# A mixture-of-experts loop on one core: W1 as the stationary operand, loaded per tile; free tags; one jump over skipped rounds; final statistics shared between two engines

## The reference

```python
x = x + attn(layernorm(x))            # 16 heads, bias table added after the softmax, then a layernorm
x = x + cross_attn(layernorm(x), ctx) # 77 context rows, 16 heads, masked
x = x + ffn(layernorm(x))
# ffn: 8 experts, top 2 of softmax(flat @ gate_W), weights normalised to sum 1
out = 0.5 * gelu(flat @ shared_W + shared_b)
for e in range(8):
    h = gelu(flat @ W1[e] + b1[e])                        # (2048,256) @ (256,1024)
    out = out + combine[:, e:e+1] * (h @ W2[e] + b2[e])   # (2048,1024) @ (1024,256)
out = layernorm(out) * gamma + beta
```

## Time and profile before

| | |
|---|---|
| median of 3 runs | 824.73 us (821.93 to 825.29) |
| profiled execution, its own time | 817.05 us |
| its span | 815.2 us |
| PE busy | 741.1 us, 91% |
| DVE, ACT, POOL busy | 363.7, 408.1, 147.5 us |
| mean granted TensorE clock | 0.97 |
| moved to and from HBM | 72.86 MB read, 42.33 MB written |

### The profile page before, as it was taken

One profiled execution on the slowest core, in us unless ns is written; L12 is line 12 of the kernel. 1 busy time (PEld: TensorE's weight loads), 2 busy tenths in 40 slices (PEclk: granted clock), 3 DMA queues, 4 the chain that ended last, 5 costly groups with the idle time before them and its releaser, 6 DMA issues.

```text
span 815.2 us, 17861 instructions
## 1 busy us (share of the span) xinstructions
PE 741.1 (91%) x6677; PEld 431.6 (53%) x6678; DVE 363.7 (45%) x1012; ACT 408.1 (50%) x514; POOL 147.5 (18%) x140
## 2 busy tenths in 40 slices
PE   4978999999999999988998899999999999999820
PEld 2444445454544444434555675767676766767520
DVE  5771220210154452588466543444444444444336
ACT  2746889887898898945564332212111121212104
POOL 2020050010000000200043340333212112121414
PEclk9997999999999999999999989999999999999975
DMA  9577939860203123036339955454444544454444
GB/s 210 148 233 192 318 89 318 277 205 23 81 2 101 39 63 99 3 113 257 117 112 317 331 213 174 102 126 111 120 120 106 123 102 126 99 130 110 73 116 103
DMA packets 81471, 116.21 MB, mean 143 GB/s; under 512 B 11202, under 2 KB 69788, under 8 KB 79066
## 3 DMA queue, kind: packets, MB, share of 16 engines
q1 hardware_dynamic: 73864, 104.27, 41.9%
q0 software_dynamic: 7536, 10.95, 7.6%
HBM read 72.86 MB, written 42.33 MB: 141 GB/s over the span
## 4 chain that ended last, share of the span: by engine, by line
PE 77%; DVE 9%; DMA 6%; ACT 4%; issue 2%; SPq 1%; POOL 1%; ACTq 0%; DVEq 0%; POOLq 0%
PE ps L1853 15%; PE ps L2195 14%; PE ps L2178 14%; PE ps L1830 14%; PE ps L2186 4%; DMA q_parts<-arena 2%; PE ps L2034 2%; DMA x_sb<-in_x 1%; PE ps L1868 1%; PE ps L1990 1%; PE ps L1812 1%; PE ps L1906 1%; DMA sums_by_row<-arena 1%; PE ps L2168 1%; PE ps L2031 1%
## 5 line engine op out<-in xcount | busy, mean ns | idle before, releaser
L847 ACT ACTIVATE arena<-ps 128x1024 f32<-128x1024 f32 x256 | 241.2, 1034 | 35.5 <-PE ps L1853 35.3
L1853 PE MATMUL ps<-arena 99*32 99x512 bf16 x2048 | 162.9, 390 | 3.2 <-issue 2.7
L1830 PE MATMUL ps<-arena 128*32 128x256 f32 x2048 | 159.6, 382 | 0.6 <-issue 0.6
L2195 PE MATMUL ps<-arena,xh_tag 128*128 x560 | 128.4, 383 | 3.0 <-DVE xh_tag L1557 3.0
L2178 PE MATMUL ps<-arena 128*128 x280 | 126.2, 593 | 0.8 <-ACT arena L958 0.5
L2195 PEld LDWEIGHTS ps<-arena,xh_tag 128*128 128x128 f32 x560 | 104.9, 192 | 16.9 <-issue 3.7
L958 ACT COPY arena<-ps 128x256 f32<-128x256 f32 x35 | 13.0, 372 | 195.9 <-PE ps L2168 195.9
L751 POOL DMA_INDIRECT sums_by_row<-arena x39 | 60.2, 1544 | 228.2 <-DVE arena L1579 226.9
L1830 PEld LDWEIGHTS ps<-arena 128*32 128x32 f32 x2048 | 65.3, 111 | 53.1 <-issue 3.3
L1552 DVE TENSOR_TENSOR xh_tag<-ps,xh_tag 128x1024 f32<-128x1024 f32 x35 | 42.9, 1225 | 88.3 <-PE ps L2178 88.3
L2178 PEld LDWEIGHTS ps<-arena 128*128 128x128 f32 x280 | 50.5, 190 | 51.5 <-issue 51.4
(11 more groups left out here) (247 smaller groups left out, 792.2 us busy)
## 6 DMA issues: line engine op xcount, KB each, us to landing
xh_tag<-in_L_ffn_b SPq DMA_DIRECT2D x35, 512.0 KB, 3.7
rows_by_expert<-arena SPq DMA_DIRECT2D x9, 1950.0 KB, 14.8
arena<-in_L_ffn_W SPq DMA_DIRECT2D x16, 1024.0 KB, 10.9
arena<-q_parts SPq DMA_DIRECT2D x90, 128.0 KB, 2.7
arena<-k_parts SPq DMA_DIRECT2D x42, 128.0 KB
q_parts<-arena SPq DMA_DIRECT2D x12, 384.0 KB, 2.5
arena<-rows_by_expert SPq DMA_DIRECT2D x35, 130.0 KB, 2.1
arena<-in_L_ffn_b SPq DMA_DIRECT2D x35, 128.0 KB, 3.0
```

The lines of the kernel that those rows point to most:

```text
L847: nc.scalar.activation(probs_of(stage, h), ps[:, 2 * (u % 2):2 * (u % 2) + 2, :].rearrange("p a n -> p (a n)"), ACT.Exp, scale=float(D) ** ...
L1830: last = nc.tensor.matmul(ps[32 * h:32 * h + 32, 4 + half, at:at + 256], v_grp[n % 2][:, kt, h, :], probs_of(stage, h)[:, 256 * part:256 * ...
L1853: last = nc.tensor.matmul(ps[c:c + 32, 2 * (u % 2) + half, :], k_stk[buf][:, h, P * st + c:P * st + c + 32], q_stk[buf][:, h, 512 * half:5 ...
L2195: last = nc.tensor.matmul(ps[:, 6, 0:D], hid_t[:, k, :], w2_sb[:, bass.ds(e, 1), k, :].squeeze(1), start=(k == 0), stop=(k == HID // P - 1))
```

## The change

W1 is no longer resident. SP loads the W1 of each tile's expert, 1 MB, into one of two buffers (`w1_buf`), as soon as `layer1` two tiles back has ended. `layer1` now takes pieces of W1 as the stationary operand and the tile's turned rows as the moving one, so that the hidden values come out already turned. `turn_hidden`, `sum_hidden` and `turned_hidden` go; b1 becomes a column per 128 hidden values, added within the gelu, which ACT does in eight pieces straight from PSUM, into two alternating `hid_t`. The per-tile broadcast of b1 goes too: all b1 are turned once (`b1_all`) and DVE copies eight columns per tile (`bias1`). `tags` no longer waits for a scatter, since the row numbers that POOL reads are copied to `row_used` in `result`. A conditional round that is not run jumps over all later ones. In front of the loop `keep_busy(1)` becomes `keep_busy(4)`, the later `keep_busy(2)` goes, and the third base store comes after the first two W1 loads. In the last stage three of the six pieces get their sums and squares from ACT's accumulating activations; DVE does the rest with two fused operations for each row tile; POOL has no part.

```diff
-        w1_sb = Region(0).take([P, EXPERTS, KC, HID])
+        r = Region(0)
+        w1_buf = r.take([P, 2, KC, HID])
+        b1_all = r.take([P, EXPERTS, HID // P])
...
             with eng.If_ne(flag, 0):
                 body(i)
+                may_run(on, eng, i + 1, body, counts)
             with eng.If_eq(flag, 0):
-                for s, before_round, step in counts(i):
-                    eng.wait_ge(s, before_round)
-                    eng.sem_inc(s, step)
+                for skipped in range(i, PAIRS):
+                    for s, before_round, step in counts(skipped):
+                        eng.wait_ge(s, before_round)
+                        eng.sem_inc(s, step)
...
-            for e in range(2, EXPERTS - 1):
-                load_w1(e)
+            sp.dma_start(b1_rows, b1.rearrange("e (k p) -> (e k) p", p=P)).then_inc(b1_in, 16)
...
-            for ch in range(3):
+            for ch in range(2):
                 store_base(ch)
...
-                sp.wait_ge(h_sum, j + 1)
-                load_b1(e, buf)
+                sp.wait_ge(h_ps, 2 * j + 2)
+                load_w1(e, buf)
...
-            sp.wait_ge(scattered, 16 * 2 * NT)
             sp.wait_ge(slot_ready, NT // CHUNK + 1)
             for j in range(2):
+                load_w1(expert(j), j)
+            store_base(2)
+            sp.wait_ge(scattered, 16 * 2 * NT)
+            for j in range(2):
                 load_rows(slots_of(j), j)
-                load_b1(expert(j), j)
...
+                add_result((n - 1) % 2, n, row_used[:, (n - 1) % 2:(n - 1) % 2 + 1], sums_set)
...
-            pool.wait_ge(x_shifted, 2 + B)
-            for n in range(LAST):
-                rows = slice(*ROUNDS[n])
-                pool.wait_ge(out_scaled, n + 1)
-                nc.gpsimd.tensor_tensor(x_sb[:, rows, :], x_sb[:, rows, :], y_in[:, rows, :], ALU.add).then_inc(out_ready, 1)
...
-            def activate(n):
-                act.wait_ge(h_sum, n)
-                nc.scalar.activation(hid, hid, ACT.Gelu).then_inc(h_act, 1)
+            def activate(buf, n, free=None):
+                act.wait_ge(b1_ready, n)
+                if free is not None:
+                    act.wait_ge(y_ps, free)
+                for half in range(2):
+                    act.wait_ge(h_ps, 2 * n - 1 + half)
+                    for c in range(4):
+                        k = 4 * half + c
+                        last = nc.scalar.activation(hid_t[:, buf, k, :], ps[:, 4 * buf + half, P * c:P * (c + 1)], ACT.Gelu,
+                                                    bias=b1_col[:, buf, k:k + 1])
+                last.then_inc(h_act, 1)
...
+            def sums(n):
+                act.wait_ge(y_landed[n], 16)
+                first, end = ROUNDS[n]
                 for t in range(first, end):
-                    last = nc.scalar.activation(y_in[:, t, :], y_in[:, t, :], ACT.Identity, scale=rstd[:, t:t + 1], bias=shift[:, t:t + 1])
-                last.then_inc(out_normed, 1)
+                    last = nc.scalar.activation(unread[:, t - first, :], y_in[:, t, :], ACT.Identity, scale=-1.0 / D, accum_out=shift[:, t:t + 1])
+                last.then_inc(out_sums, 1)
+                n_sums[0] += 1
+            def squares(n):
+                act.wait_ge(out_sums, n_sums[0])
+                first, end = ROUNDS[n]
+                for t in range(first, end):
+                    last = nc.scalar.activation(unread[:, t - first, :], y_in[:, t, :], ACT.Square, bias=shift[:, t:t + 1], accum_out=mv[:, t, 1:2])
...
+            act.wait_ge(y_ps, SLOT_TILES)
+            root_of_vector(1, 0)
+            sums(1)
+            root_of_vector(2, 2)
+            squares(1)
+            sums(3)
+            squares(3)
+            root_of_vector(3, 5)
+            sums(4)
+            squares(4)
...
+            def bias1(buf, tile, read=None):
+                e = nc.vector.value_load(tile_expert[0:1, tile], min_val=0, max_val=EXPERTS - 1)
+                if read is not None:
+                    dve.wait_ge(h_act, read)
+                nc.vector.tensor_copy(b1_col[:, buf, :], b1_all[:, bass.ds(e, 1), :].squeeze(1)).then_inc(b1_ready, 1)
...
-                    dve.wait_ge(sums_set, 16 * taken)
...
+                if keep_rows:
+                    nc.vector.tensor_copy(row_used[:, buf:buf + 1], row_at[:, buf:buf + 1])
...
-                    turned_hidden(2 * i + (o + 2))
-                    sum_hidden(o, 2 * i + (o + 3), 16 * i + 32)
-                    tags(o, 2 * i + (o + 3), bass.ds(2 * i + (o + 2), 1), 2 * i + (o + 1),
-                         min(2 * i + (o + 1), 2 * SURE + 1) if may_be_skipped else 2 * i + (o + 1))
+                    bias1(o, bass.ds(2 * i + (o + 2), 1), 2 * i + (o + 1))
+                    dve.wait_ge(xs_ps, 2 * i + (o + 3))
+                    tags(o, 2 * i + (o + 3), bass.ds(2 * i + (o + 2), 1), 2 * i + (o + 1))
...
+            def centred(n, roots=None):
+                if roots is not None:
+                    dve.wait_ge(ln_std, len(LN_TILES) + roots + 1)
+                else:
+                    dve.wait_ge(ln_var, len(LN_TILES) + 1 + D_ROUNDS.index(n) + 1)
+                for t in range(*ROUNDS[n]):
+                    middle, op = (shift[:, t:t + 1], ALU.add) if n in BY_SCALAR else (mv[:, t, 0:1], ALU.subtract)
+                    last = nc.vector.scalar_tensor_tensor(out=y_in[:, t, :], in0=y_in[:, t, :], scalar=middle, in1=ffn_g_sb, op0=op, op1=ALU.mult)
+                link(last)
...
+            def added(n, roots):
...
+                dve.wait_ge(ln_std, len(LN_TILES) + roots + 1)
+                link(nc.vector.reciprocal(rstd[:, rows], rstd[:, rows]))
+                for t in range(*ROUNDS[n]):
+                    last = nc.vector.scalar_tensor_tensor(out=x_sb[:, t, :], in0=y_in[:, t, :], scalar=rstd[:, t:t + 1], in1=x_sb[:, t, :],
+                                                          op0=ALU.mult, op1=ALU.add)
+                last.then_inc(out_scaled, 1)
...
+            dve.wait_ge(x_shifted, 2 + B)
             variances(0)
-            for n in range(LAST):
-                variances(n + 1)
-                scales(n)
-                if n >= 1:
-                    gains(n - 1).then_inc(out_scaled, 1)
-            scales(LAST)
-            gains(LAST - 1).then_inc(out_scaled, 1)
-            link(gains(LAST))
-            rows = slice(*ROUNDS[LAST])
-            dve.wait_ge(x_shifted, 2 + B)
-            nc.vector.tensor_tensor(x_sb[:, rows, :], x_sb[:, rows, :], y_in[:, rows, :], ALU.add).then_inc(out_scaled, 1)
+            centred(0)
+            variances(2)
+            added(0, 1)
+            centred(2)
+            added(2, 2)
+            centred(1, 3)
+            added(1, 3)
+            variances(5)
+            centred(5)
+            centred(3, 4)
+            added(3, 4)
+            added(5, 5)
+            centred(4, 6)
+            added(4, 6)
...
-            def layer1(j, buf, ready, summed=None):
-                e = nc.tensor.value_load(tile_expert[0:1, bass.ds(j, 1)], min_val=0, max_val=EXPERTS - 1)
+            def layer1(buf, ready, landed, read=None):
                 pe.wait_ge(xs_ready, ready)
-                if summed is not None:
-                    pe.wait_ge(h_sum, summed)
+                pe.wait_ge(w1_landed[buf], landed)
+                if read is not None:
+                    pe.wait_ge(h_act, read)
                 for half in range(2):
-                    for k in range(KC):
-                        last = nc.tensor.matmul(ps[:, half, :], xs_t[:, buf, k, :],
-                                                w1_sb[:, bass.ds(e, 1), k, 512 * half:512 * (half + 1)].squeeze(1),
-                                                start=(k == 0), stop=(k == KC - 1))
-                last.then_inc(h_ps, 1)
-            def turn_hidden(n):
+                    for c in range(4):
+                        at = P * (4 * half + c)
+                        for k in range(KC):
+                            last = nc.tensor.matmul(ps[:, 4 * buf + half, P * c:P * (c + 1)], w1_buf[:, buf, k, at:at + P], xs_t[:, buf, k, :],
+                                                    start=(k == 0), stop=(k == KC - 1))
+                    last.then_inc(h_ps, 1)
...
+            def layer2(e, n, buf, taken=None):
                 pe.wait_ge(h_act, n)
-                for k in range(HID // P):
-                    last = nc.tensor.transpose(ps[:, 4 + k // 4, P * (k % 4):P * (k % 4 + 1)], hid[:, P * k:P * (k + 1)], ident[:, :])
-                last.then_inc(ht_ps, 1)
...
-            pe.wait_ge(w1_in, 16 * EXPERTS)
             pe.wait_ge(w2_in, 16 * EXPERTS)
-            keep_busy(1, 5, sgw_sb[:, :, 0:D])
+            keep_busy(4, 4, sgw_sb[:, :, 0:D])
+            pe.wait_ge(b1_set, 1)
             turn_tile(0, 16)
-            layer1(0, 0, 1)
+            layer1(0, 1, 16)
             turn_tile(1, 16, 1)
-            keep_busy(2, 5, sgw_sb[:, :, 0:D])
-            turn_hidden(1)
```

(20 more changed lines are left out.)

164 lines of the change are left out of this document (73 added, 91 removed).

## The result

The changed kernel takes 797.32 us (median of four, 793.05 to 798.58) against 824.73 us (four, 821.93 to 825.29): ratio 0.9673, 95% interval 0.9636 to 0.9711. 798.2 us was forecast. The profiled execution took 796.49 us with a span of 794.6 us at a mean granted clock of 0.968.

The account below looks back on a forecast made before the run. PE, without gaps in the expert loop, was taken as the bound. Savings of 24.0 (loop), 0 (entry), 1.5 (behind the loop) and 1.0 (last stage) sum to 26.5 us: 824.73 to 798.2 us, range 792 to 813.

Parts of the forecast that it names:

- Loop, -24.0 forecast: Expert loop: transposes go, layer 1's 32 load-matmul pairs take 111 ns each; step 7.23 us, 24.0 us less over 32 steps.
- Rival A: Layer 1: weight loads show, 134 ns a pair, step 7.97 us, loop gains 0.4, total 822 us; 8%.
- W1 by DMA, 0: Loop: W1's load per tile lands in about 2.6 plus 2 us, with 10.9 us available; nothing priced in.
- rival B: Loop: W1 lands late, showing from 10.4 us; at 14 us a step takes 9.0, total about 855 us; 6%.
- had cost nothing in the loop: Loop: the wait that tags loses was free, since PE had no gap.
- Scatters: Loop: each lands 3.8 us after issue, 6.4 with 1 MB in front, and still fits the 7.23 us step.
- rival C: Loop: the scatter chain lengthens to 7.6 us under W1's traffic and sets the step; total 810 us; 5%.
- Entry, 0: Loop entry: with four fillers and first layer 1 at 494.4, timing ends at 506.05 against 506.06; change 0.
- rows and W1 have landed by then: Loop entry: first rows and W1 are in place when the four fillers end at 493.5 us.
- Behind the loop, -1.5 forecast: After the loop: last layer 2 may start at about 775.1 instead of 776.32; 1.5 us less, bounds 1 and 3.4.
- the scatter chain stays: After the loop: POOL's scatters still end the wait, the last dummy landing and freeing the result at 774.22 us.
- Last stage, -1 forecast: Final statistics and outputs: DVE's work falls from 19.0 to about 18 us; 1 us less, bounds 3 less and 1 more.

Follow-up runs that it names:

- run 1: Changed kernel with layer 1 moving only 64 of each tile's 128 tokens: 801.27 us, one execution.
- run 9: The changed kernel unchanged, measured again on the chip of two later runs: 791.51 us against 817.03 for the kernel before, ratio 0.9682.
- run 4: Changed kernel with the tags' wait for the scatter put back and the row-number copy removed: 820.92 us, one execution; the kernel before took 821.75.
- run 8: Changed kernel with one filler at the loop's entry instead of four: 791.58 us, ratio 0.9708.
- run 10: Changed kernel with both first W1 loads moved ahead of the second base store and one filler at the entry: 791.01 us, ratio 0.9696.
- Run 11: run 10 plus closing expert numbers loaded behind the last layer 1 and y's pieces loaded in output order: 790.48 us, ratio 0.9684.
- runs 5 to 9: Changed kernel with old last stage, rounds tested singly, later expert numbers, one filler, and unchanged: 792.83, 793.27, 791.09, 791.58, 791.51 us.
- run 12: Run 11 with only the first W1 load ahead, the second behind both row loads, and three fillers: 790.16 us against 817.53, ratio 0.9634.
- Run 7: Changed kernel with PE's two expert-number loads for the closing layer 2 moved behind the last layer 1: 791.09 us, ratio 0.968.
- run 5: Changed kernel with the last stage of the kernel before (DVE takes all statistics, POOL adds): 792.83 us, ratio 0.9699.
- runs 6 to 10: Changed kernel with rounds tested singly, later expert numbers, one filler, unchanged, and W1 loads earlier with one filler: 793.27, 791.09, 791.58, 791.51, 791.01 us.
- runs 1 to 4: Changed kernel, one execution each: half the moving columns, W1 loaded twice, three times, tags' wait put back: 801.27, 809.62, 877.46, 820.92 us.

## Why the prediction was right

- **Loop, -24.0 forecast, -23.6 measured.** Right in mechanism and size: 111 ns a pair was the term, 111.5 came, and run 1 shows that the moving columns don't set it. 3.57 + 0.22 + 3.46 = 7.25 against 7.23. The rule of the Trainium skill ("TensorE: Matmul & The Clock Gate", Back-to-back issue gap) gives, as an estimate from its 81 and 56 ns for a pair and for a matmul alone, pairs 25 ns further apart; it isn't borne out here for float32 with 128 columns. The step by that estimate was 7.97 us. Rival A is out. The prediction's "No row here has this pair" was too strict: the transposes that the change removes are each a 128x128 load and a matmul of 128 columns, at 109 ns a pair, and only their load is shorter, 141 ns against 192 in layer 2. The row of before on that load:

```profile
L2186 PEld LDWEIGHTS ps<-ident,xh_tag 128*128 128x128 f32 x280 | 32.6, 141 | 7.3 <-issue 2.7 <-ACT xh_tag L962 1.3
```

- **W1 by DMA, 0, and rival B.** Right. The prediction put a landing at 4.6 us (2.6 plus 2) and lateness at 10.4; in run 9, the same kernel, the loop's W1 loads landed after 6.3 us in the median and 7.8 at most. Twice the bytes still fit the settled step.
- **The tags' wait: "had cost nothing in the loop".** True of the kernel before and the wrong question. In the new loop it is worth (7.90 - 7.245) x 32 = 21 us (run 4), because a scatter that is issued close behind W1's load needs 5.8 us to land and not 3.8, and the ring through the tags adds 2.2 to that. The sum came out right since the change included it; a reader who took the edit for idle and left it out would have got 820.92 us.
- **Scatters, rival C.** 3.9 us to landing in the loop, and DVE's result waits there for PE and for no scatter; C is out. The prediction's own bound of 6.4 us for a scatter behind 1 MB was near: 5.8 in run 4, which is what C would have looked like. What it left out is the 2.2 us that follow the landing.
- **Gelu on ACT, 2.5 us hidden.** 2.18 + 0.37, hidden.
- **Entry, 0: +0.1 from the first filler on, but the step "rows and W1 have landed by then" failed.** The rows came 17.0 us behind the slots (480.35 to 497.36) instead of 13.1 (475.45 to 488.56). Without the three more fillers at that place it would have cost 3.4 us (run 8). Counted from the slots to the third layer 1, the entry costs 1.5 us in this profile (32.2 against 30.6) and 0.8 in run 9. What holds the rows' load back is the landing of the last scatter of rows, 5.5 us after its issue in this profile (489.80 to 495.29) instead of 2.5, with the DMA engines at 374 to 419 GB/s from 492 to 498 us. Runs 10 and 11 didn't help (16.7 and 16.5 us, against 16.3 to 17.4 in the changed kernel and runs 5 to 9), since the W1 loads can't be issued much sooner; in run 12 one load was enough to slow the last four scatters, and it was 16.1. An order that puts both W1 loads behind the rows was not tried.
- **Behind the loop, -1.5 forecast, -2.1 measured, for another reason.** The forecast's step was "the scatter chain stays". It is 1 us shorter than PE's own way, which was not costed: three serial value loads and the semaphore steps. Run 7 takes two of them off the path and the scatter bound appears. With the same code, or nearly, this stretch, from the last step's layer 1, was 33.5 to 35.3 us in six profiles, mostly by whether the last layer 1 took 5.3 or 6.7 us; by that the gain lies between 0.8 and 2.6 us, against the one profile of before. The forecast's own times also give 1.2 us and not 1.5 (775.1 against 776.32).
- **Last stage, -1 forecast, -1.3 measured.** DVE's stretch was to shrink from 19.0 to 18 and grew to 19.7 (771.07 to 790.81); what shrank is what follows its last operation, 5.8 to 3.8 us. Why that tail shrank stays open; run 5, with the old last stage, has 5.8 us again. So the size is luck here: the forecast had the saving in DVE's stretch. Of the 1.7 us above the forecast 1.57 are a wait that it did not see (at 774.60 us): DVE's second block is the third that is loaded. In runs 6 to 10, with the same last stage, it was 0.5 to 2.0 us, and the stage's gain lies between 1.0 and 2.5 us. Run 11 removes the wait.

The nearness of the total, 0.9 us, is luck beyond the loop's term: executions of one program differ more, and on the chip of run 9 the same two kernels lay 25.5 us apart (817.03 and 791.51), where 26.5 was forecast and 27.4 measured first. The start of the fillers at the entry lay anywhere from 484.4 to 496.4 us in nine profiles (the changed kernel and runs 5 to 12), whose programs are the same up to there, or nearly, and up to 500.8 in runs 1 to 4. In runs 10 and 11, the earliest, the clock didn't fall between 80 and 490 us; in the profile after it did from 422 us for 10 us and again from 480 for 3.

## What to carry to other kernels

A wait is priced in the loop that will be, not in the one that is: write down every ring of waits with its length under the new traffic and compare it with the new step. Here a ring of about 6.1 us, which cost nothing at a step of 7.98, became one of 8.1 beside the loads that the change adds, and took back nearly all that the change gives. When an engine is the bound, ask next what its own sequence holds between two blocks of work (value loads, semaphore steps), and whether it can be issued under the work ahead. Load what is consumed in the order in which it is consumed; where an engine must wait for data, filler work can be worth the clock it keeps (3.4 us here). And when a reordering does nothing, look first whether it moved the transfer at all: run 10's moved by one microsecond.

## What the runs showed of the hardware

A full float32 weight load and a matmul of 128 columns overlap entirely: 111.5 ns a pair, 110 with half of the columns. Indirect scatters of 128 rows slow down beside a load of 1 MB: from about 2.5 us to landing to between 5.9 and 6.7 at the entry (run 12), from 3.9 to 5.8 in the loop when they are issued 0.8 us behind it (run 4). Three loads of a value on PE's sequencer stood about 0.8 us apart and aren't hidden unless matmuls are queued ahead of them; under layer 1 they cost nothing (run 7). After an idle time of 3.17 us layer 1 took 6.18 us, after 4.0 to 4.5 us 5.3 to 6.7, after 2.57 us once 3.81; but 2.72 and 2.93 us (runs 12 and 11) were followed by 5.36 and 5.44. The DMA engines held 375 GB/s over 100 us, beside PE at a clock of 0.93.
